# A decoder layer on one core: the order of work inside a cross-attention slot, and one or two more PSUM banks for its side products

## The reference

```python
q = (text_hidden @ Wq)...; k = (vision_tokens @ Wk)...; v = (vision_tokens @ Wv)...   # 16 heads of 128, 8 kv heads
scores = jnp.einsum('bhtd,bhsd->bhts', q, k) / scale
attn = jax.nn.softmax(jnp.where(mask, scores, -jnp.inf), axis=-1)
out = jnp.einsum('bhts,bhsd->bhtd', attn, v)
return out.transpose(0, 2, 1, 3).reshape(B, T_text, N_HEADS * HEAD_DIM) @ Wo
...
x = x + cross(layernorm(x), ctx)
x = x + experts(layernorm(x))     # gate logits, top 2, softmax of the two, silu(h0) * h1, wo
```

## Time and profile before

| | us |
|---|---|
| median of 3 runs | 924.18 (923.66 to 924.8) |
| the profiled execution | 926.15 |
| span of its instructions | 924.4 |
| PE busy in the span | 862.0 (93%) |
| DVE, ACT, POOL busy | 532.2, 454.0, 271.0 |

### The profile page before, as it was taken

How to read it: one execution, slowest core, us unless ns; L and a number is a source line. 1 busy time by engine, 2 the same in 40 slices (tenths; PEclk the granted TensorE clock), 3 DMA queues, 4 the chain that set the end, 5 groups by cost and what they waited for, 6 DMA issues and landing times.

```text
span 924.4 us, 16031 instructions
## 1 busy us (share of the span) xinstructions
PE 862.0 (93%) x5373; PEld 746.6 (81%) x5374; DVE 532.2 (58%) x1579; ACT 454.0 (49%) x1210; POOL 271.0 (29%) x397
## 2 busy tenths in 40 slices
PE   8899999999999999998888999989768999999995
PEld 7788888898888888887667777877767788888874
DVE  5676666565666656564767758868856532232231
ACT  4776666666666666665424335442443522322221
POOL 1333322332233222332021211603561322323222
PEclk9999999999999999999999999999979999999998
DMA  8001996000000000020000000205771333333322
GB/s 318 1 2 64 300 314 175 1 1 1 2 1 1 23 1 1 1 91 2 24 0 2 10 14 1 70 1 175 251 275 53 47 52 50 49 49 51 52 46 29
DMA packets 46019, 60.15 MB, mean 65 GB/s; under 512 B 2816, under 2 KB 37760, under 8 KB 45824
## 3 DMA queue, kind: packets, MB, share of 16 engines
q1 hardware_dynamic: 38208, 47.83, 16.8%
q0 software_dynamic: 7744, 11.44, 6.8%
HBM read 30.65 MB, written 28.61 MB: 64 GB/s over the span
## 4 chain that ended last, share of the span: by engine, by line
PE 83%; DVE 8%; ACT 4%; issue 2%; DMA 2%; another core or an unknown queue 0%; POOLq 0%; POOL 0%; SPq 0%; DVEq 0%
PE bank_y L1757 7%; PE bank_o L47 5%; PE bank_y L47 5%; PE bank_y L49 5%; PE bank_y L48 5%; PE bank_q L47 5%; PE bank_s L47 4%; PE bank_q L48 4%; PE bank_q L49 4%; PE bank_o L49 4%; PE bank_t L495 4%; PE bank_o L48 4%; PE bank_s L49 4%; PE bank_s L48 4%; PE bank_s L487 3%; PE bank_o L1748 2%
## 5 line engine op out<-in xcount | busy, mean ns | idle before, releaser
L289 POOL TENSOR_TENSOR a_prob<-a_prob,a_rinv 128x128 f32<-128x128 f32 (+1 forms) x256 | 124.6, 508 | 296.9 <-DVE a_rinv L382 294.7
L357 DVE TENSOR_TENSOR a_pT_lo<-bank_t,a_pT_hi 128x384 fp32r<-128x384 f32 x128 | 70.5, 550 | 101.7 <-ACT a_pT_hi L305 101.7
L318 ACT ACTIVATE a_prob<-a_masked,a_negmax 128x128 f32<-128x128 f32 (+1 forms) x256 | 114.9, 461 | 0.0
L305 ACT ACTIVATE a_pT_hi<-bank_t 128x384 fp32r<-128x384 f32 x128 | 62.9, 491 | 104.9 <-PE bank_t L495 104.9
L1115 POOL DMA_INDIRECT out_dram<-b_y,b_rows x39 | 62.8, 1611 | 159.0 <-DVE b_y L1526 155.7
L415 DVE CUSTOM_DVE_ANT_0 a_masked<-bank_s,a_causal 128x128 f32<-128x128 f32 (+1 forms) x256 | 80.2, 350 | 7.5 <-PE bank_s L49 7.5
L1519 DVE TENSOR_TENSOR b_xT_lo<-bank_o,b_xT_hi 128x256 fp32r<-128x256 f32 x39 | 16.5, 424 | 117.9 <-ACT b_xT_hi L1231 117.9
L1757 PE MATMUL bank_y<-b_We,b_interT 128*128 x312 | 75.4, 384 | 2.2 <-issue 1.3
L47 PE MATMUL bank_y<-a_WprojT_hi,a_oT_hi 128*128 128x256 f32 x256 | 72.5, 283 | 0.6 <-DVE a_oT_lo L357 0.6
L357 DVE TENSOR_TENSOR a_oT_lo<-bank_o,a_oT_hi 128x512 fp32r<-128x512 f32 x64 | 44.3, 692 | 49.1 <-ACT a_oT_hi L305 49.1
L49 PE MATMUL bank_y<-a_WprojT_hi,a_oT_lo 128*128 128x256 f32 x256 | 72.2, 282 | 0.0
(11 more groups left out here) (346 smaller groups left out, 2433.9 us busy)
## 6 DMA issues: line engine op xcount, KB each, us to landing
slots<-a_nobody SPq DMA_DIRECT2D x1, 16641.0 KB, 63.9
b_W<-in_L_ffn_w_kernel_dram SPq DMA_DIRECT2D x16, 512.0 KB, 4.4
b_rows<-slots SPq DMA_DIRECT2D x39, 129.0 KB
b_We<-in_L_ffn_wo_kernel_dram SPq DMA_DIRECT2D x8, 512.0 KB
a_stage<-n_L_attn_weight_qkv_dram SPq DMA_DIRECT2D x5, 512.0 KB, 7.5
x_WqT<-in_L_xattn_Wq_dram SPq DMA_DIRECT2D x1, 2048.0 KB, 8.5
b_wo<-in_L_xattn_Wo_dram SPq DMA_DIRECT2D x1, 2048.0 KB, 9.2
x_WqT<-_L_attn_weight_proj_dram SPq DMA_DIRECT2D x3, 512.0 KB, 11.6
```

Source lines behind the costliest of these rows:

```text
L289: pool.tensor_tensor(prob[:, u % 3, a:b], prob[:, u % 3, a:b], rinv[:, u % 4, i:i + 1].to_broadcast([P, b - a]), ALU.mult)\
L305: act.activation(dst.hi, src, ACT.Copy).then_inc(half[n], 1)
L318: act.activation(prob[:, u % 3, a:b], masked[:, u % 2, a:b], ACT.Exp, scale=-1.0, bias=negmax[:, u % 4, i:i + 1], accum_out=rowsum[:, u % ...
L357: dve.tensor_tensor(dst.lo, src, dst.hi.bitcast(F32), ALU.subtract).then_inc(free[n], 1)
```

## The change

Only the order and the banks of slots in which a next pair is being prepared change (pairs 0 to 2, and slot (3,0)); `fills_first` names them. There PE makes scores, all fills except rt and rank, outputs of tile t-2, then rt and rank, then the transposes. The bank set for the fills of such a slot gains o0, and at t = 3 o0 and o1. The gate logits of pairs 0 and 1 move from the end of slot (p,2) to the head of the fills of slot (p,3). ACT copies the first two fills ahead of the exponential and the others behind it. DVE takes the shift, the low parts of up to four fills, the row sum, the other low parts, and only then the residual with its statistics, the low parts of the transposed probabilities and the shift vector of the layer norm. No matmul, copy or DMA is added or taken away.

```diff
-        if 1 <= p < PAIRS and t == 2:
-            fills = [("rt", p - 1, c) for c in range(HC)] + fills if part == 0 else fills + [("gate", p - 1, 0)]
+        if 1 <= p < PAIRS and (t, part) == (2, 0):
+            fills = [("rt", p - 1, c) for c in range(HC)] + fills
+        if 1 <= p < PAIRS and (t, part) == ((3, 0) if p + 1 < PAIRS else (2, 1)):
+            fills = [("gate", p - 1, 0)] + fills
...
+    def fills_first(p, t):
+        return p + 1 < PAIRS or (p, t) == (PAIRS - 1, 0)
+    def early_fills(p, t):
+        return [name for part in range(2) for name in fills_at(p, t, part) if name[0] not in ("rt", "rank")]
+    def late_fills(p, t):
+        return [name for part in range(2) for name in fills_at(p, t, part) if name[0] in ("rt", "rank")]
...
+    def fill_banks(p, t):
+        more = () if not fills_first(p, t) else ("o0", "o1") if t == 3 else ("o0",)
+        return ROT[t % 2] + more
...
-        for i, name in enumerate(fills_at(p, t, 0) + fills_at(p, t, 1)):
-            use_fill(name, ROT[t % 2], i)
+        for i, name in enumerate(early_fills(p, t) + late_fills(p, t) if fills_first(p, t) else
+                                 fills_at(p, t, 0) + fills_at(p, t, 1)):
+            use_fill(name, fill_banks(p, t), i)
...
+                early = early_fills(p, t) if fills_first(p, t) else []
+                for name in early[:2]:
+                    high(name)
                 if p < PAIRS:
                     act.wait_ge(shifted, 2 * (p * TT + t + 1))
                     act.activation(prob[:, t % 2, :], prob[:, t % 2, :], ACT.Exp, scale=SCALE).then_inc(exp_done, 1)
...
+                if fills_first(p, t):
+                    for name in early[2:] + late_fills(p, t):
                         high(name)
+                    tile_highs(p, t)
...
+                if fills_first(p, t):
+                    early = early_fills(p, t)
+                    for name in early[:4]:
+                        low(name)
+                    softmax_sum(p, t)
+                    for name in early[4:]:
+                        low(name)
+                    if earlier_tile(p, t, 2):
+                        residual(*earlier_tile(p, t, 2))
+                        group_stats(*earlier_tile(p, t, 2))
+                    tile_lows(p, t)
+                    if packs_at(p, t) is not None:
+                        group_shift(packs_at(p, t))
...
                 if p < PAIRS:
                     scores(p, t)
+                if fills_first(p, t):
+                    for name in early_fills(p, t):
+                        fill(name)
                 if earlier_tile(p, t, 2):
                     outputs(*earlier_tile(p, t, 2))
+                if fills_first(p, t):
+                    for name in late_fills(p, t):
+                        fill(name)
+                    if earlier_tile(p, t, 1):
+                        transposes(*earlier_tile(p, t, 1))
```

More of the change, by code:

```diff
@@ L1475, in _ @@
                     softmax_shift(p, t)
-                if earlier_tile(p, t, 2):
-                    residual(*earlier_tile(p, t, 2))
-                    group_stats(*earlier_tile(p, t, 2))
-                if p < PAIRS:
+                if fills_first(p, t):
[11 more added lines that the diff above has]
+                        group_shift(packs_at(p, t))
+                else:
+                    if earlier_tile(p, t, 2):
+                        residual(*earlier_tile(p, t, 2))
+                        group_stats(*earlier_tile(p, t, 2))
+                    if p < PAIRS:
+                        if t < 3:
+                            softmax_sum(p, t)
+                        for name in fills_at(p, t, 0):
+                            low(name)
+                        if (p, t) == (PAIRS - 1, 3):
+                            tile_lows(p, t)
+                        if t == 3:
+                            softmax_sum(p, t)
@@ L1495, in _ @@
-                if t == 3 and p < PAIRS - 1:
-                    tile_lows(p, t)
+                    if packs_at(p, t) is not None:
+                        group_shift(packs_at(p, t))
+                    if p < PAIRS:
+                        for name in fills_at(p, t, 1):
+                            low(name)
+                    if t == 3 and p < PAIRS - 1:
+                        tile_lows(p, t)
                 if p + 1 < PAIRS:
@@ L1711, in _ @@
                     scores(p, t)
+                if fills_first(p, t):
+                    for name in early_fills(p, t):
+                        fill(name)
                 if earlier_tile(p, t, 2):
                     outputs(*earlier_tile(p, t, 2))
-                for name in fills_at(p, t, 0):
-                    fill(name)
-                if t < 3 and earlier_tile(p, t, 1):
-                    transposes(*earlier_tile(p, t, 1))
-                if (p, t) == (PAIRS, 1):
-                    keep_busy(pe, bank[IT_BANK][:, 0:P], ident[:], 16)
-                for name in fills_at(p, t, 1):
-                    fill(name)
-                if t == 3:
-                    transposes(*earlier_tile(p, t, 1))
+                if fills_first(p, t):
[3 more added lines that the diff above has]
+                        transposes(*earlier_tile(p, t, 1))
+                else:
+                    for name in fills_at(p, t, 0):
+                        fill(name)
+                    if t < 3 and earlier_tile(p, t, 1):
+                        transposes(*earlier_tile(p, t, 1))
+                    if (p, t) == (PAIRS, 1):
+                        keep_busy(pe, bank[IT_BANK][:, 0:P], ident[:], 16)
+                    for name in fills_at(p, t, 1):
+                        fill(name)
+                    if t == 3:
+                        transposes(*earlier_tile(p, t, 1))
             keep_busy(pe, bank[IT_BANK][:, 0:P], ident[:], 36)
```

29 lines of the change are left out of this document (9 added, 20 removed).

## The result

The changed kernel takes 907.2 us as the median of four runs (905.55 to 915.5), the kernel before beside it 924.49; the ratio is 0.983, 95% interval 0.980 to 0.986. On a second chip, with six runs, it was 908.67 against 923.9, ratio 0.982 (0.979 to 0.985). The forecast was 905.7 us with a range of 900 to 917, and the time lies inside it.

The account below looks back on a forecast made before the run. PE was taken to set the pace, standing still about 18 us, mostly for low parts that DVE subtracts. Savings per slot summed to 18.5 us, taking the profiled execution from 926.15 to 907.6 and the median to 905.7, range 900 to 917.

Parts of the forecast that it names:

- The dense slots: Slots where PE never waits: 10.7 us for (1,0), 10.6 for (1,1), 16.9 for (1,3), 15.05 for (0,3).
- the ring through o0: Transposes, fills, exponential and DVE wait on each other in a circle through bank o0; rivals had it return gain or set pace.
- the rivals of 912 and 930: Half the gain comes back through o0 and POOL (912, chance 0.22); late DVE delays transposes, making the kernel slower (930, 0.07).
- The wait of 3.8: Slot (0,1): transposes wait 3.8 us for the v fill on o0, until 476.15; slow clock behind it costs 1.6 us.
- The premise that waits of 1.2 to 1.6 cost no clock: PE waits of 1.2 to 1.6 us bring no slow clock, since slots holding them showed clock 1.00.
- 13.25 twice: Slots (1,2) and (2,2): late layer norm makes rt wait 0.3 and transposes 1.1 us, so 13.25 instead of 11.7.
- the 0.6 us that the prediction set aside for the exclusive lock: Slots (0,1), (1,1), (2,1): if POOL's multiplication blocks DVE's variance, the power comes 0.6 us later; total 907 to 908.
- The gates: Gate logits of pairs 0 and 1 directly behind dense scores keep clock 1.00, gaining 1.7 us twice.
- The tail: Stretch from slot (3,1) on: old order, no gain counted, at most 3 us as upper bound.
- The sign that named 64.5: From (3,1) to the first expert tile should take the same 64.5 us as before.
- the cover of outputs and transposes (3.8 us): Outputs and transposes between the fills and next scores give 3.8 us in which copies and subtractions fit.
- the rival in which the waits only change place: Each wait ahead of scores becomes an equal one ahead of the transposes; 924.2 us, within 0.2%, chance 0.04.

Follow-up runs that it names:

- filler: Changed kernel with 14 identity matmuls keeping PE busy inside the wait ahead of the transposes in slot (0,1); 902.82 us, ratio 0.980.
- before_again: The kernel before, unchanged, profiled a second time; 923.51 us against 922.73 beside it, one run.
- mult_waits: both_ahead, with POOL at t=1 multiplying only behind DVE's normalization or the group's shift vector, and storing behind that; 897.83 us, ratio 0.971.
- both_ahead: Changed kernel with, at t=1, the next layer norm moved first on DVE and POOL and all four ACT fill copies ahead of the exponential; 904.53 us, ratio 0.981.
- gate_behind: Changed kernel with the gate logits of pairs 0 and 1 back behind the transposes of (1,2) and (2,2), banks kept; 913.23 us, ratio 0.988.
- order_alone: Changed kernel with the new order but the three fill banks of before, no o0 and o1; 923.43 us, ratio 1.000.
- gate_alone: Kernel before with only the gate logits of pairs 0 and 1 moved to the head of the fills of (p,3); 918.99 us, ratio 0.994.

## Why the prediction was right, and where it was not

**The dense slots.** 10.7, 10.6, 16.9 and 15.05 us were forecast for (1,0), (1,1), (1,3) and (0,3); 10.74, 10.53, 16.74 and 14.97 came. The prices of PE's pieces from the earlier trace rows carried the sum to 0.2 us a slot. No M fill waits at t=3, and no transposes at t=0 in pairs 1 and 2: the ring through o0 does not set the pace, and the rivals of 912 and 930 fall.

**Where the missing 2.6 us are.** The slots (0,1) and (0,2) gave 1.35 us less than forecast and (1,2) and (2,2) 1.5 less; the others together came out 0.3 better.

**The slow clock in (0,1) and (0,2).** The wait of 3.8 was forecast to its end (476.15 against 476.14), but its price was taken as 1.6 us, all of it in (0,2). filler shows 2.5: 0.8 at the transposes themselves and 1.75 in (0,2). So slot (0,1) saved 0.25 instead of 0.95. (0,2) took 12.77 instead of 12.1, most of that because it takes 11.02 and not 10.5 without the slow clock. The premise that waits of 1.2 to 1.6 cost no clock fell too: behind the three of (0,1) in before_again the clock is 0.50 and (0,2) takes 14.14 us, where it took 12.57 in the earlier trace rows. Those rows held no proof of it either: they show the clock of (0,2), not that of (0,1), and 0.91 behind the wait of 1.42.

**Slots (1,2) and (2,2)** took 13.70 and 14.25 instead of 13.25 twice. In (1,2) the waits are as forecast:

```profile
529.26 2.40 DVE L1293 TENSOR_SCALAR b_ln_var<-b_ln_mv 128x4 f32<-128x4 f32 x1
529.71 1.91 POOL L1113 TENSOR_TENSOR b_prob<-b_prob,b_rinv 128x1024 f32<-128x1024 f32 x1
531.74 1.03 POOL L1026 TENSOR_TENSOR b_ln_rstd<-b_ln_var,b_minus_half 128x4 f32<-128x4 f32 x1
532.80 1.38 DVE L1298 TENSOR_SCALAR b_xn<-x_all,b_ln_mv,b_ln_rstd 128x256 f32<-128x256 f32 x4 [1.14 <-POOL b_ln_rstd L1026]
534.10 0.68 DVE L1307 TENSOR_REDUCE b_rowmax<-bank_q 128x8 f32<-128x512 f32 x1
...
537.23 1.25 PE L1656 MATMUL bank_s<-x_ident,b_packed_z 128*128 128x128 f32 x8 [0.38 <-DVE b_VW_lo L1273]
```

with 1.14 ahead of the transposes; the shift starts 7.4 us in (7.1 forecast). What was missing is the price of a wait beyond its row: against the 11.61 us of mult_waits, which has no wait there, (1,2) takes 2.09 more with 1.52 of waits and (2,2) 2.64 more with 2.07, so 0.29 on average for each of the four waits; what the time goes into is not shown. In (2,2) rt waits 0.94 instead of 0.3, because the group's shift vector, 4 elements, took 2.77 us beside store and multiplication, and POOL waited 0.60 for DVE's variance before the power:

```profile
580.74 2.77 DVE L1354 SCALAR_TENSOR_TENSOR b_g_shift<-b_g_mv,b_g_rstd 128x4 f32<-128x4 f32 x1
581.56 1.92 POOL L1113 TENSOR_TENSOR b_prob<-b_prob,b_rinv 128x1024 f32<-128x1024 f32 x1
584.09 1.01 POOL L1026 TENSOR_TENSOR b_ln_rstd<-b_ln_var,b_minus_half 128x4 f32<-128x4 f32 x1 [0.60 <-DVE b_ln_var L1293]
```

That is the 0.6 us that the prediction set aside for the exclusive lock (the Trainium skill, SBUF — State Buffer, "SBUF: two separate sides"), in one of the three slots named, though it was the shift vector and not the variance that was held. In (1,1) the variance was caught (2.40 us), but the power behind it had to queue behind the multiplication anyway; in (0,1) it was not caught. By mult_waits the trace agrees with that rule: four normalizations from SBUF to SBUF take 1.38 us again when POOL does not multiply beside them (2.96 in both_ahead). It is not every such operation: the shift vector of slot (1,1), which began 0.08 us behind POOL's store, took 0.16 us. The rule was weighed as a fault of 0.6 us; used as a tool it gave the largest single step behind the changed kernel, 4.9 us.

**The gates.** No low clock behind those of pairs 0 and 1, as forecast, and gate_behind prices the place at 3.2 us, 3.4 in the forecast. The reason given was wrong: that little idle time ahead of the gate (0.26 us) leaves the clock alone. It fell behind the gate of pair 2, and in gate_behind with none. In before_again it stayed up behind the wait of 1.42, so for pair 1 part of the gain hangs on an execution in which it fell.

**The tail.** Nothing was given for the way behind (3,1), and nothing is there: 61.2 to 61.4 us in both kernels, once the accident in the profile of before is known. The sign that named 64.5 was built on that accident.

**Small slips in the working.** The 13.25 of t=2 is 0.15 more than its parts (11.7, 0.3 and 1.1). DVE's work in the earlier trace rows is 8.8 to 11.5 us in slots of 11.5 to 18.9, not 9.4 to 11.5 in slots of 12.5 and more. At 552.0 the scores of (1,3) end; the clock is back at 1.00 before 551. None of them moves the forecast by more than 0.3 us.

**What no term named.** The forecast took the cover of outputs and transposes (3.8 us) as the work of the order, and never priced the banks apart. order_alone is, almost to the number, the rival in which the waits only change place, which had a chance of 0.04: without o0 the waits go ahead of the fourth fill. The sum came out because order and banks were made together; that the working never asked which of the two it needed is the luck in it.

## What to carry to other kernels

When work is moved up so that its copies are hidden, count the banks that it now holds at once: a reorder without the bank moved the wait from one matmul to another here. Ask of each early operation what will run beside it: the normalizations of DVE, moved beside POOL's multiplication, took twice as long and gave back part of what the move had won. A deliberate wait on the engine that has time can be the cheaper order. And where PE must stand still for microseconds, compare with a version that keeps it busy, because the wait in the row was not the whole price here (2.5 us beyond 3.66).

## What the runs showed of the hardware

- Four normalizations of 128x256 on DVE: 1.38 us alone, 2.96 beside a POOL multiplication, 4.00 beside POOL's DMA issue and multiplication. Operations of 4 elements took 2.40 and 2.77 us there, and one 0.16. Maxima and subtractions that read a bank stayed at 0.68 us.
- The granted clock behind the same piece of program is not the same in each execution: behind the three waits of slot (0,1) in the kernel before it was 1.00 once and 0.50 twice (before_again, gate_alone), at a price of 1.56 us; behind the wait of 3.66 us the price was 2.5 in two executions and 1.2 in two others. Two kernels should not be compared by one slot that holds such a wait.
- Four short waits of PE, 0.38 to 1.14 us, cost 0.29 us each on average beyond their length in the row.
- One profiled execution can hold a late start of 3.3 us on two engines that no second one shows.
- What makes the changed kernel scatter (903.7 to 915.5 in its ten runs), when mult_waits with the filler stays within 1.7 us, was not settled; a clock that falls in some executions, in (0,1), behind the gate of pair 2 and at the last outputs, is the candidate, but the execution of 915.5 us has no profile.
